# Normalization on GpSimd in a loop of 30 steps: one two-input subtraction for two groups, one multiply for a group, and the bias matmul in one piece

## The chip, the cores and the metric

The kernel runs on one core of a Trainium2 chip. The metric is the device time of one execution in microseconds. Single runs are told by their median; the profile comes from one execution of its own.

## The reference, cut to what matters

The input x is 16 graphs of 512 nodes with 128 channels, float32. Three layers of graph work (normalization, aggregation, a feed-forward product, convolution, message passing and a gated update) come first. Then the last layer runs 30 steps on all 8,192 rows, and it is this loop that the change touches:

```python
def step(h, _):
    h = h + 0.01 * jnp.tanh(h)
    h = h * jax.nn.sigmoid(h)
    h = _layernorm(h, ln_w, ln_b)      # (h - mean) * rsqrt(var + 1e-5) * w + b, over 128 channels
    h = jnp.einsum('bsc,dc->bsd', h, W) + b
    return (h, None)
x, _ = jax.lax.scan(step, x, None, length=N_ITERS)   # 30
```

The result is added to x.

## The kernel before, in words

**Stages.** The graph layers work through the 16 graphs one after the other, in three interleaved phases (`steps`). The first groups of the loop are begun inside the last graph's steps. Then comes the loop itself (`slots`): the 8,192 rows are cut into 64 tiles of 128 rows by 128 channels; eight tiles are a group (`GT`, 1,024 columns on 128 partitions), and eight groups are all the data. One slot is one group of one iteration, 240 slots in all.

**A group's way round.** TensorE multiplies the eight tiles by the weight (`product_group`, L890) into two banks of PSUM. ScalarE takes the tanh (L1010), VectorE forms h + 0.01 tanh(h) (L1326), ScalarE applies the silu and writes the group into its own buffer of `g_ring` (L1000), VectorE gathers sums and squares of each row (`statistics_of`, L1309) and, for two groups at a time, a reciprocal root by a chain of small instructions (`root_link`, L1363 to L1397), whose last one writes `f_rs`. GpSimd normalizes the group from `g_ring` into `h_ring` (`scale`). TensorE transposes the eight tiles (L942), and ScalarE copies them back to SBUF for the next product (L1014).

**Order.** Every engine has its own written order of work per slot. The engines trail one another by fixed lags in groups: the silu by one (`LAG_S`), the negated means by four (`LAG_M`), the scaling by five (`LAG_P`), the transposes by six (`LAG_T`). `h_ring` has four buffers and `f_rs` two. Semaphores (`f_bn`, `f_root`, `f_mean`, `f_norm`, `f_turn`, ...) carry the hand-overs.

**What GpSimd does for a group.** `PLAIN` = 2 of the four tiles in each half of a group are only multiplied by the reciprocal root, in one two-input instruction of 256 columns whose second operand is a column of `f_rs` repeated over 128 channels (L525). The other two tiles of the half take one instruction each (L528): add the negated mean, multiply by the root, both being values per partition. The negated means of two groups come from `less_mean` (L512) once in two slots, ahead of the scaling. After each half the semaphore `f_norm` is raised, so a group raises it twice.

**How the mean of the plain tiles is taken off.** The tiles that were not centred go through the plain weight `w1_t`, whose row for the last channel is used for the bias, and the others through a weight `w1c_t`. The bias of the plain tiles comes in by a matmul in bf16 ahead of the product (`bias`, L906): the bias is split in three bf16 parts in the rows of `bias1`, 256 columns for each half. The centred tiles are transposed with 127 rows, and a row of ones, written once by `ones_row` at the beginning, carries their bias.

**TensorE's slot.** Product of group k; wait for the first half of the group six behind (`f_norm`); two transposes, bias of the first half, two transposes; wait for the second half; two transposes, bias of the second half, two transposes.

Of the kernel before, what the change touches and what calls it, by code (L numbers as in the profile page):

```python
# [27 lines left out]
P = 128  # L28
# [27 lines left out]
EARLY = 7  # L56
PLAIN = 2

# [34 lines left out]
def build(nc, x, adj, w0, b0, wf, bf, w_se, b_se, conv1_w, bn1, conv2_w, bn2, w_msg, b_msg,  # L93
          w_ih, b_ih, w_hh, b_hh, ln_w, ln_b, w1, b1, out):
    with ExitStack() as ctx:
# [17 lines left out]
        f_rs = sb("f_rs", [P, 2, PAIR])  # L113
        f_less = sb("f_less", [P, GROUPS, GT])
        f_share = sb("f_share", [P, PAIR])
# [81 lines left out]
        u_ring = [sb(f"u_ring{r}", [P, GN])[:] for r in range(2)]  # L197
        g_ring = [sb(f"g_ring{r}", [P, GN])[:] for r in range(4)]
        h_ring = [sb(f"h_ring{r}", [P, GN])[:] for r in range(4)]
        g_ring += [sb(f"g_ring{r}", [P, GN])[:] for r in range(4, GROUPS)]  # L200

# [199 lines left out]
        def both(j):  # L401

            return j // 2 % 2

        def pairs(i, j):

            return i * (GROUPS // 2) + j // 2 - BY_POWER // 2
# [54 lines left out]
        def _(pool):  # L462
# [44 lines left out]

            def less_mean(j, s):

                pool.wait_ge(f_bn, s + 2)  # L510
                settle(pool, s_passed_pool)
                pool.tensor_scalar(f_less[:, j:j + 2, :], f_stat[:, j:j + 2, 0, :, 1], -1.0, 1.0,  # L512
                                   ALU.mult, ALU.mult).then_inc(f_mean, 1)

            def scale(i, j, s):
                if isinstance(i, int) and i == 0 and j < BY_POWER:
                    pool.wait_ge(f_pow, j + 1)
                else:
# [12 lines left out]

            def slot(it, k):
                older = earlier(it, k, LAG_M)
                if older is not None and k % 2 == 0:
                    less_mean(*older[1:])
                before = earlier(it, k, LAG_P)
                if before is not None:
                    scale(*before)

            def step(b, p, c, d):  # L540
# [39 lines left out]
                if ends(b, B):  # L580
                    power(2)
                    power(3)
                    less_mean(2, 2)
                if l1:
# [8 lines left out]
                if ends(b, B - 1):  # L593
                    rstd(3, b - 1)
                    power(0)
                    less_mean(0, 0)
                    scale(0, 0, 0)
                    power(1)
                    scale(0, 1, 1)
# [15 lines left out]
        def _(pe):  # L615
# [288 lines left out]

            def bias(k, h):
                pe.matmul(y_ps[(k + 1) % 2][:, h, 0:PLAIN * C], ones_bf[:],  # L906
                          bias1[:, 0:PLAIN, :].rearrange("p t c -> p (t c)"),
                          start=True, stop=False, skip_group_check=True)

            def ones_row(b):  # L910

                for t in range(0, NT, NT - PLAIN):
                    pe.matmul(bank[b][:, C * t:C * t + C * (NT - PLAIN)], ones_bf[:],
                              bias1[:, PLAIN:NT, :].rearrange("p t c -> p (t c)"), start=(t == 0), stop=True,
                              skip_group_check=True)

            def slot(it, k):
# [4 lines left out]
                if before is not None:  # L922
                    i, j, s = before
                    if ends(i, 0) and j == 0:
                        pe.wait_ge(s_conv_pre, B)
                        ones_row(CONV)
                        pe.wait_ge(s_x_nmp_lo, B)
                        ones_row(CHAN)
                    elif ends(i, 0) and j == 1:
                        pe.wait_ge(s_r, B)  # L930
                        ones_row(DIST_A)
                    else:
                        pe.wait_ge(f_state, s - 1)
                    pe.wait_ge(f_norm, 2 * s + 1)
                for n in range(GT):
                    if before is not None:
                        if n == NT:
                            pe.wait_ge(f_norm, 2 * s + 2)
                            wait(pe, f_state, s)
                        t = (n + NT * (j % 2)) % GT  # L940
                        rows = P if t % NT < PLAIN else P - 1
# [204 lines left out]
        def _(dve):  # L1146
# [15 lines left out]
            link(dve.memset(bias1[:], 0.0))  # L1162
            dve.memset(bias1[0:1, PLAIN:NT, :], 1.0)
            dve.memset(b1_cols, 0.0)
# [77 lines left out]
            def split_bias():  # L1242
# [5 lines left out]
                link(dve.tensor_copy(part_bf[:, 2, :], part_f[:, 2, :]))  # L1248
                for t in range(PLAIN):
                    for r in range(3):  # L1250
# [120 lines left out]
            def root_link(n, i, j, s):  # L1371
# [22 lines left out]
                else:  # L1394
                    dve.wait_ge(f_link, done)
                    dve.wait_ge(f_norm, 2 * s - 4)
                    dve.scalar_tensor_tensor(out=f_rs[:, both(j), :], in0=f_share[:], scalar=LESS[2],  # L1397
# [219 lines left out]
```

## Time and profile before

| | us |
|---|---|
| Median of three runs | 1288.19 (1287.89 to 1288.37) |
| The profiled execution's own time | 1290.16 |
| Its span, first to last instruction | 1288.3 |

The profile counts for each engine the time it is busy (PE is TensorE's matmuls, PEld its weight loads, DVE VectorE, ACT ScalarE, POOL GpSimd). Times of single instructions are in nanoseconds where they stand as a mean, otherwise in microseconds. The span leaves out what lies around the instructions. In the loop the granted clock of TensorE is 1.00, its upper level.

### The profile page before, as it was taken

How to read it: one execution, taken by the hardware profiler on the slowest of the kernel's cores; microseconds unless marked ns; L12 is line 12 of the kernel's file. 1: busy time of each engine (PE TensorE's matmuls, PEld its weight loads, DVE VectorE, ACT ScalarE, POOL GpSimd, SP SyncE). 2: the span in 40 equal slices, each digit the busy share in tenths (PEclk: the TensorE clock that was granted, in tenths of full speed). 3: DMA queues.
4: the chain of work that ended last, by engine and by line, in shares of the span. 5: the costliest groups of instructions: out<-in, count | busy, mean ns of one | idle time of the engine just before them, and what ended most of it. 6: DMA issues, size and time to landing. Idle time of an engine off the chain costs nothing.

```text
span 1288.3 us, 30559 instructions
## 1 busy us (share of the span) xinstructions
PE 1250.8 (97%) x9315; PEld 1111.1 (86%) x9315; DVE 1156.3 (90%) x3029; ACT 960.1 (75%) x1170; POOL 991.9 (77%) x1867
## 2 busy tenths in 40 slices
PE   8899999999999999789999999999999999999998
PEld 7677777777777777589999999999999999999998
DVE  7888888888888877889999999999999999999996
ACT  2455555555555555789999999999999999999994
POOL 3455555554555554699999999999999999999997
PEclk9999999999999999889999999999999999999999
DMA  6111111111111000000000000000000000000004
GB/s 192 42 42 44 52 52 53 45 41 41 41 41 41 0 1 1 1 2 1 0 0 0 0 0 0 0 0 0 0 0 0 0 0 0 0 0 0 0 0 131
DMA packets 29811, 27.75 MB, mean 22 GB/s; under 512 B 3285, under 2 KB 21464, under 8 KB 29656
## 3 DMA queue, kind: packets, MB, share of 16 engines
q1 hardware_dynamic: 29784, 27.41, 6.6%
q8 instruction: 15, 0.25, 0.1%
q14 instruction: 12, 0.10, 0.0%
HBM read 23.21 MB, written 4.19 MB: 21 GB/s over the span
## 4 chain that ended last, share of the span: by engine, by line
PE 39%; DVE 5%; issue 5%; POOL 4%; ACT 2%; DVEq 0%; POOLq 0%; ACTq 0%
PE psum L890 24%; PE psum L942 13%; POOL h_ring L528 3%; PE psum L906 3%; ACT t_ring L1010 2%; DVE f_stat L1309 2%; POOL h_ring L525 1%; DVE u_ring L1326 1%; DVE f_share L1363 1%; DVE psum L1368 1%; DVE psum L1379 0%; DVE psum L1382 0%; DVE f_rs L1397 0%; DVEq L1307 0%; DVEq L1320 0%
## 5 line engine op out<-in xcount | busy, mean ns | idle before, releaser
L528 POOL TENSOR_SCALAR h_ring<-g_ring,f_less,f_rs 128x128 f32<-128x128 f32 x960 | 428.1, 457 | 0.0
L1309 DVE BATCH_NORM_STATS2 f_stat<-g_ring 128x6 f32<-128x256 f32 x960 | 393.6, 424 | 2.4 <-ACT g_ring L1000 2.4
L942 PE MATMUL psum<-ident,h_ring 128*128 128x128 f32 (+1 forms) x1920 | 339.6, 279 | 9.6 <-POOL h_ring L528 9.4
L525 POOL TENSOR_TENSOR h_ring<-g_ring,f_rs 128x256 f32<-128x256 f32 x480 | 296.1, 617 | 17.5 <-DVE f_rs L1397 15.4
L1326 DVE SCALAR_TENSOR_TENSOR u_ring<-t_ring,psum 128x1024 f32<-128x1024 f32 x232 | 282.9, 1219 | 28.2 <-ACT t_ring L1010 27.0
L890 PE MATMUL psum<-w_t,y_all 128*128 128x128 f32 x1920 | 293.7, 276 | 0.0
L890 PE MATMUL psum<-w1c_t,y_all 128*128 128x128 f32 x1920 | 293.7, 276 | 0.0
L942 PEld LDWEIGHTS psum<-ident,h_ring 128*128 128x128 f32 (+1 forms) x1920 | 254.2, 167 | 43.4 <-POOL h_ring L528 17.0
L1010 ACT ACTIVATE t_ring<-psum 128x1024 f32<-128x1024 f32 x232 | 237.7, 1025 | 43.1 <-PE psum L890 42.8
L1014 ACT ACTIVATE y_all<-psum 128x1024 f32<-128x1024 f32 x240 | 244.0, 1017 | 15.9 <-PE psum L942 15.9
L890 PEld LDWEIGHTS psum<-w1c_t,y_all 128*128 128x128 f32 x1920 | 253.9, 193 | 0.0
L890 PEld LDWEIGHTS psum<-w_t,y_all 128*128 128x128 f32 x1920 | 253.3, 192 | 0.0
L1000 ACT ACTIVATE g_ring<-u_ring 128x1024 f32<-128x1024 f32 x240 | 251.7, 1049 | 0.6 <-DVE u_ring L1326 0.5
L906 PE MATMUL psum<-bias,ones_bf 65*128 65x256 bf16 x480 | 131.8, 275 | 0.0
L495 POOL TENSOR_SCALAR ln_ve<-ln_stat 128x4 f32<-128x4 f32 x64 | 19.4, 303 | 132.1 <-DVE ln_stat L1261 132.1
L996 ACT ACTIVATE work<-psum 128x512 f32<-128x512 f32 x64 | 34.7, 595 | 96.2 <-PE psum L757 96.1
L675 PE MATMUL psum<-diff_s_h,wt_h 128*128 128x256 f32 x272 | 81.2, 299 | 0.0
L676 PE MATMUL psum<-diff_s_l,wt_h 128*128 128x256 f32 x272 | 76.4, 281 | 0.0
L677 PE MATMUL psum<-diff_s_h,wt_l 128*128 128x256 f32 x272 | 76.3, 280 | 0.0
L497 POOL TENSOR_TENSOR ln_rs<-ln_ve,half_neg 128x4 f32<-128x4 f32 x64 | 71.7, 1120 | 5.3
L501 POOL TENSOR_TENSOR work<-work 128x512 f32<-128x512 f32 x32 | 46.5, 1455 | 32.7 <-DVE xh_mem L1292 25.5
L1363 DVE TENSOR_REDUCE f_share<-psum 128x16 f32<-128x48 f32 x354 | 67.5, 191 | 0.1
(201 smaller groups left out, 2189.8 us busy)
## 6 DMA issues: line engine op xcount, KB each, us to landing
work<-in_adj_dram SPq DMA_DIRECT2D x16, 1024.0 KB, 5.5
x_tok<-in_x_dram SPq DMA_DIRECT2D x16, 256.0 KB, 5.6
out_dram<-y_all SPq DMA_DIRECT2D x7, 512.0 KB, 3.2
work<-in_L_gnn_conv_w_dram SPq DMA_DIRECT2D x1, 1088.0 KB
out_dram<-y_all SPq DMA_DIRECT2D x2, 256.0 KB, 3.6
work<-in_L_gnn_w_ih_dram SPq DMA_DIRECT2D x1, 384.0 KB
work<-in_L_gnn_w_hh_dram SPq DMA_DIRECT2D x1, 192.0 KB
work<-in_L_gnn_W_dram SPq DMA_DIRECT2D x1, 64.0 KB, 5.1
```

The source lines that it names most:

```text
L525: pool.tensor_tensor(tiles(h_ring[j % 4])[:, first:first + PLAIN, :], tiles(g_ring[j])[:, first:first + PLAIN, :], spread(f_rs[:, both(j), ...
L528: ins = pool.tensor_scalar(tiles(h_ring[j % 4])[:, t, :], tiles(g_ring[j])[:, t, :], f_less[:, j, t:t + 1], f_rs[:, both(j), at + t:at + t ...
L675: pe.matmul(dst, lhs[0], rhs[0], start=start, stop=False)
L890: m = pe.matmul(y_ps[k % 2][:, h, C * t:C * t + C], y_all[:, GT * k + NT * h + t, :], w1_t[:] if t < PLAIN else w1c_t[:], start=False, sto ...
L906: pe.matmul(y_ps[(k + 1) % 2][:, h, 0:PLAIN * C], ones_bf[:], bias1[:, 0:PLAIN, :].rearrange("p t c -> p (t c)"), start=True, stop=False, ...
L942: m = pe.transpose(g_ps[j % 2][0:rows, t // NT, P * (t % NT):P * (t % NT) + P], tiles(h_ring[j % 4])[:, t, 0:rows], ident[:])
L1000: act.activation(g_ring[j], u_ring[j % 2], ACT.Silu).then_inc(f_silu, 1)
L1010: act.activation(t_ring[k % 2], src, ACT.Tanh).then_inc(f_tanh, 1)
L1014: act.activation(y_all[:, GT * j:GT * j + GT, :].rearrange("p t c -> p (t c)"), g_ps[j % 2].rearrange("p h n -> p (h n)"), ACT.Copy).then_ ...
L1309: ins = dve.bn_stats(f_stat[:, j, 0, 2 * q:2 * q + 2, :].rearrange("p t w -> p (t w)"), two)
L1326: dve.scalar_tensor_tensor(out=u_ring[k % 2], in0=t_ring[k % 2], scalar=STEP, in1=src, op0=ALU.mult, op1=ALU.add).then_inc(f_u, 1)
L1363: dve.tensor_reduce(f_share[:], rows, AX_X, ALU.mult).then_inc(f_link, 1)
```

## The change

Two things are changed, and the buffers and weights with them.

- GpSimd now centres one half (four tiles, 512 columns) of each group by a subtraction of the mean in place in `g_ring`, for two groups in one instruction (`centre`): the first half of the even group and the second half of the odd one. The mean comes straight from the statistics, repeated over the channels; the buffer and the instruction of the negated means go. Then one multiply covers a whole group of 1,024 columns (`scale`), and `f_norm` is raised once per group. In its slot the scaling comes first, the centring second. The buffers of two groups now lie side by side (`g_pair`), so that one access reaches both halves.
- In TensorE's slot the half that was not centred gets its bias in one matmul of 512 columns (the two rows of tiles of `bias1` read twice), between the fourth and the fifth transpose. The centred half is transposed first, with 127 rows. The wait for GpSimd is one per group, ahead of the first transpose.

```diff
-        g_ring = [sb(f"g_ring{r}", [P, GN])[:] for r in range(4)]
+        g_pair = [sb(f"g_pair{r}", [P, 2, GN]) for r in range(2)]
...
+        g_ring = [g_pair[j // 2][:, j % 2, :] for j in range(GROUPS)]
...
-            def less_mean(j, s):
+            def centre(j, s):
                 pool.wait_ge(f_bn, s + 2)
-                settle(pool, s_passed_pool)
-                pool.tensor_scalar(f_less[:, j:j + 2, :], f_stat[:, j:j + 2, 0, :, 1], -1.0, 1.0,
-                                   ALU.mult, ALU.mult).then_inc(f_mean, 1)
+                two = g_pair[j // 2][:].rearrange("p g n -> p (g n)").rearrange("p (q n) -> p q n", n=N)[:, 0:4:3, :] \
+                    .rearrange("p g (t c) -> p g t c", c=C)
+                means = f_stat[:].rearrange("p g o t w -> p (g o t) w")[:, :, 1].rearrange("p (q t) -> p q t", t=NT)[:, 4 * j:4 * j + 6:5, :] \
+                    .rearrange("p g (t o) -> p g t o", o=1).broadcast_to([P, 2, NT, C])
+                pool.tensor_tensor(two, two, means, ALU.subtract).then_inc(f_mean, 1)
...
-                for h in (j % 2, 1 - j % 2):
-                    first = NT * h
-                    at = GT * (j % 2)
-                    pool.tensor_tensor(tiles(h_ring[j % 4])[:, first:first + PLAIN, :], tiles(g_ring[j])[:, first:first + PLAIN, :],
-                                       spread(f_rs[:, both(j), at + first:at + first + PLAIN], PLAIN, C), ALU.mult)
-                    for t in range(first + PLAIN, first + NT):
-                        ins = pool.tensor_scalar(tiles(h_ring[j % 4])[:, t, :], tiles(g_ring[j])[:, t, :],
-                                                 f_less[:, j, t:t + 1], f_rs[:, both(j), at + t:at + t + 1], ALU.add, ALU.mult)
-                    ins.then_inc(f_norm, 1)
+                at = GT * (j % 2)
+                pool.tensor_tensor(tiles(h_ring[j % 4]), tiles(g_ring[j]),
+                                   spread(f_rs[:, both(j), at:at + GT], GT, C), ALU.mult).then_inc(f_norm, 1)
...
-                older = earlier(it, k, LAG_M)
-                if older is not None and k % 2 == 0:
-                    less_mean(*older[1:])
                 before = earlier(it, k, LAG_P)
                 if before is not None:
                     scale(*before)
+                newer = earlier(it, k, LAG_M)
+                if newer is not None and k % 2 == 0:
+                    centre(*newer[1:])
...
-                                      w1_t[:] if t < PLAIN else w1c_t[:], start=False, stop=True, skip_group_check=True)
+                                      w1c_t[:] if h == centred(k) else w1_t[:], start=(h == centred(k) and t == 0), stop=True, skip_group_check=True)
...
-            def bias(k, h):
-                pe.matmul(y_ps[(k + 1) % 2][:, h, 0:PLAIN * C], ones_bf[:],
-                          bias1[:, 0:PLAIN, :].rearrange("p t c -> p (t c)"),
+            def bias(k):
+                four = bias1[:, 0:2, :].rearrange("p (o t) c -> p o (t c)", o=1).broadcast_to([KB, 2, 2 * C])
+                pe.matmul(y_ps[k % 2][:, 1 - centred(k), :].rearrange("p (o n) -> p o n", o=2), ones_bf[:], four,
                           start=True, stop=False, skip_group_check=True)
...
-                    pe.wait_ge(f_norm, 2 * s + 1)
+                    pe.wait_ge(f_norm, s + 1)
...
-                    if ahead and n % NT == 1:
-                        if n == 1:
-                            bias_free(it, k)
-                        bias(k, n // NT)
+                    if ahead and n == NT - 1:
+                        bias_free(it, k)
+                        bias((k + 1) % GROUPS)
```

`centred(j)` is `j % 2`. The remaining lines fit the counts of `f_norm` to one per group (VectorE's last link of the root waits for `s - 2` instead of `2 * s - 4`) and the rows of ones to the new layout.

## Rows read from the trace of the kernel before

**Rows 1.** The page's first part: busy time, share of the span and instructions of each engine.
```profile
PE 1250.8 (97%) x9315; PEld 1111.1 (86%) x9315; DVE 1156.3 (90%) x3029; ACT 960.1 (75%) x1170; POOL 991.9 (77%) x1867
```

**Rows 2.** Busy time per engine in three stretches, PEclk the granted TensorE clock.
```profile
core 0: us, PE busy (x) PEld busy (x) DVE busy (x) ACT busy (x) POOL busy (x), PEclk, DMA share, GB/s
500.00:540.00 40.00, 31.50 (x167) 24.22 (x165) 30.32 (x53) 31.23 (x43) 22.76 (x26) 0.98 0.00 1
880.00:904.44 24.44, 24.25 (x211) 23.11 (x210) 23.57 (x74) 23.01 (x25) 23.89 (x53) 1.00 0.00 0
904.44:928.88 24.44, 24.25 (x211) 23.12 (x210) 23.54 (x74) 22.99 (x25) 23.90 (x53) 1.00 0.00 0
```

**Rows 3.** Who waited for whom, 700 to 1100 us: total us, times, longest.
```profile
POOL h_ring L525 <- DVE f_rs L1397: 8.0, 27, 0.4
PEld psum L942 <- POOL h_ring L528: 9.9, 37, 0.4
```

**Rows 4.** Timeline of GpSimd, 916 to 926 us: start us, us, engine line op, tiles.
```profile
916.05 0.21 POOL L512 TENSOR_SCALAR f_less<-f_stat 128x16 f32<-128x16 f32 x1
916.22 0.62 POOL L525 TENSOR_TENSOR h_ring<-g_ring,f_rs 128x256 f32<-128x256 f32 x1
916.82 0.89 POOL L528 TENSOR_SCALAR h_ring<-g_ring,f_less,f_rs 128x128 f32<-128x128 f32 x2
...
922.01 0.21 POOL L512 TENSOR_SCALAR f_less<-f_stat 128x16 f32<-128x16 f32 x1
...
925.49 0.61 POOL L525 TENSOR_TENSOR h_ring<-g_ring,f_rs 128x256 f32<-128x256 f32 x1 [0.38 <-DVE f_rs L1397]
```

**Rows 5.** The chain that ended last, one group on TensorE: start us, us, what.
```profile
907.86 1.79 PE psum L890 x16
909.64 0.22 PE psum L942 x2
909.86 0.11 PE psum L906
909.97 0.44 PE psum L942 x4
910.42 0.11 PE psum L906
910.53 0.22 PE psum L942 x2
```

**Rows 6.** Groups of instructions by shape on GpSimd, whole span: xcount, busy us, mean ns.
```profile
L528 POOL TENSOR_SCALAR h_ring<-g_ring,f_less,f_rs 128x128 f32<-128x128 f32 x960 | 428.1, 457 | 0.0
L525 POOL TENSOR_TENSOR h_ring<-g_ring,f_rs 128x256 f32<-128x256 f32 x480 | 296.1, 617 | 17.5 <-DVE f_rs L1397 15.4 <-issue 1.7 <-POOL f_less L512 0.3
L512 POOL TENSOR_SCALAR f_less<-f_stat 128x16 f32<-128x16 f32 x120 | 25.5, 213 | 0.2
L592 POOL TENSOR_TENSOR x_conv_l<-conv_pre,x_conv_h 128x512 fp32r<-128x512 f32 x16 | 20.9, 1306 | 20.2 <-ACT conv_pre L1103 20.2
L551 POOL TENSOR_TENSOR xh_mem<-h_full 128x257 f32<-128x257 f32 x32 | 19.4, 627 | 49.8 <-ACT h_full L1040 43.8 <-DVE xs L1432 6.0
```

**Rows 7.** Timeline of GpSimd in the graph layers: pairs of 257 and of 512 columns.
```profile
197.65 1.19 POOL L551 TENSOR_TENSOR xh_mem<-h_full 128x257 f32<-128x257 f32 x2 [2.63 <-ACT h_full L1040]
201.62 2.63 POOL L558 TENSOR_TENSOR emb_f<-emb_f 105x512 f32<-105x512 f32 x2 [0.75 <-ACT emb_f L1051]
```

**Rows 8.** Groups of matmuls by shape on TensorE: 256 and 512 columns.
```profile
L676 PE MATMUL psum<-diff_s_l,wt_h 128*128 128x256 f32 x272 | 76.4, 281 | 0.0
L676 PE MATMUL psum<-xc_s_l,wt_h 128*128 128x512 f32 x64 | 25.2, 393 | 0.0
```

**Rows 9.** Timeline of GpSimd where the loop begins and where it ends.
```profile
547.26 1.64 POOL L506 TENSOR_TENSOR f_rs<-f_var,half_neg 128x8 f32<-128x8 f32 x1 [0.84 <-DVE f_var L1350]
548.99 0.72 POOL L512 TENSOR_SCALAR f_less<-f_stat 128x16 f32<-128x16 f32 x1
...
1278.08 0.90 POOL L528 TENSOR_SCALAR h_ring<-g_ring,f_less,f_rs 128x128 f32<-128x128 f32 x2
```

More of the change, by code:

```diff
@@ L56 @@
 EARLY = 7
-PLAIN = 2
 SEED_SLOPE = -0.5
@@ L113, in build @@
         f_rs = sb("f_rs", [P, 2, PAIR])
-        f_less = sb("f_less", [P, GROUPS, GT])
         f_share = sb("f_share", [P, PAIR])
@@ L197, in build @@
         u_ring = [sb(f"u_ring{r}", [P, GN])[:] for r in range(2)]
-        g_ring = [sb(f"g_ring{r}", [P, GN])[:] for r in range(4)]
+        g_pair = [sb(f"g_pair{r}", [P, 2, GN]) for r in range(2)]
         h_ring = [sb(f"h_ring{r}", [P, GN])[:] for r in range(4)]
-        g_ring += [sb(f"g_ring{r}", [P, GN])[:] for r in range(4, GROUPS)]
+        g_pair += [sb(f"g_pair{r}", [P, 2, GN]) for r in range(2, GROUPS // 2)]
+        g_ring = [g_pair[j // 2][:, j % 2, :] for j in range(GROUPS)]
         psum = ctx.enter_context(nc.psum_tensor("psum", [P, 8, N], F32))
@@ L403, in both, with centred @@
             return j // 2 % 2
+        def centred(j):
+            return j % 2
         def pairs(i, j):
@@ L582, in step @@
                     power(3)
-                    less_mean(2, 2)
+                    centre(2, 2)
                 if l1:
@@ L595, in step @@
                     power(0)
-                    less_mean(0, 0)
+                    centre(0, 0)
                     scale(0, 0, 0)
@@ L903, in bias_free @@
                     pe.wait_ge(f_u, it * GROUPS + k)
-            def bias(k, h):
-                pe.matmul(y_ps[(k + 1) % 2][:, h, 0:PLAIN * C], ones_bf[:],
-                          bias1[:, 0:PLAIN, :].rearrange("p t c -> p (t c)"),
+            def bias(k):
+                four = bias1[:, 0:2, :].rearrange("p (o t) c -> p o (t c)", o=1).broadcast_to([KB, 2, 2 * C])
+                pe.matmul(y_ps[k % 2][:, 1 - centred(k), :].rearrange("p (o n) -> p o n", o=2), ones_bf[:], four,
                           start=True, stop=False, skip_group_check=True)
             def ones_row(b):
-                for t in range(0, NT, NT - PLAIN):
-                    pe.matmul(bank[b][:, C * t:C * t + C * (NT - PLAIN)], ones_bf[:],
-                              bias1[:, PLAIN:NT, :].rearrange("p t c -> p (t c)"), start=(t == 0), stop=True,
+                for t in range(0, NT, 2):
+                    pe.matmul(bank[b][:, C * t:C * t + 2 * C], ones_bf[:],
+                              bias1[:, 2:4, :].rearrange("p t c -> p (t c)"), start=(t == 0), stop=True,
                               skip_group_check=True)
@@ L926, in slot @@
                         ones_row(CONV)
-                        pe.wait_ge(s_x_nmp_lo, B)
-                        ones_row(CHAN)
                     elif ends(i, 0) and j == 1:
@@ L937, in slot @@
                         if n == NT:
[L938 to L941, printed above, removed]
+                            if ends(i, 0) and j == 0:
+                                pe.wait_ge(s_x_nmp_lo, B)
+                            else:
+                                pe.wait_ge(f_state, s)
+                        t = (n + NT * centred(j)) % GT
+                        rows = P - 1 if n < NT else P
                         m = pe.transpose(g_ps[j % 2][0:rows, t // NT, P * (t % NT):P * (t % NT) + P],
                                          tiles(h_ring[j % 4])[:, t, 0:rows], ident[:])
-                    if ahead and n % NT == 1:
-                        if n == 1:
-                            bias_free(it, k)
-                        bias(k, n // NT)
+                    if ahead and n == NT - 1:
+                        bias_free(it, k)
+                        bias((k + 1) % GROUPS)
                 if before is not None:
@@ L1162, in _ @@
             link(dve.memset(bias1[:], 0.0))
-            dve.memset(bias1[0:1, PLAIN:NT, :], 1.0)
+            dve.memset(bias1[0:1, 2:4, :], 1.0)
             dve.memset(b1_cols, 0.0)
@@ L1248, in split_bias @@
                 link(dve.tensor_copy(part_bf[:, 2, :], part_f[:, 2, :]))
-                for t in range(PLAIN):
+                for t in range(2):
                     for r in range(3):
@@ L1395, in root_link @@
                     dve.wait_ge(f_link, done)
-                    dve.wait_ge(f_norm, 2 * s - 4)
+                    dve.wait_ge(f_norm, s - 2)
                     dve.scalar_tensor_tensor(out=f_rs[:, both(j), :], in0=f_share[:], scalar=LESS[2],
```

## The prediction

> **What bounds the kernel now.** I began with the busy shares [rows 1]. TensorE leads with 97%, but that is a mean over two stages, so I went on to the stretches of the second stage, the loop of 30 iterations [rows 2]. One iteration of eight groups lasts 24.44 us, the same in both stretches shown. In it TensorE is busy 24.25 us, GpSimd 23.90, VectorE 23.54 and ScalarE 22.99. Four engines stand within 6% of one another, so the loop is bound by whichever is slowed first, and no single one can be made faster for much gain.
>
> GpSimd's own timeline shows how little it has to spare. From one L512 at 916.05 to the next at 922.01, with no wait between them, are 5.96 us: that is all GpSimd does for two groups [rows 4]. Four times 5.96 are 23.84 us of the 24.44. The remaining 0.6 us is idle time, mostly before L525, where it waits for VectorE's f_rs: 8.0 us in 400, up to 0.38 us at once [rows 3, 4]. Two groups may take 24.44 / 4 = 6.11 us, so GpSimd's slack is 0.15 us per pair of groups, 2.5%.
>
> TensorE's part is read from the chain: 1.79 us of products, 0.88 us of transposes (0.22 + 0.44 + 0.22), and twice 0.11 us of bias make 2.89 us per group, 23.1 per iteration [rows 5]. The rest of its 24.44 us is waiting that the profile partly shows, for L528 of GpSimd among others [rows 3]. The question is therefore what GpSimd's work for two groups becomes.
>
> **What goes and what comes on GpSimd.** For two groups the change takes away the 5.96 us just read: one f_less (L512), four two-input multiplies of 256 columns (L525, a mean of 617 ns) and eight one-input instructions of 128 columns (L528, a mean of 457 ns) [rows 4, 6]. From start to start an L525 costs 0.60 us (916.22 to 916.82) [rows 4]. It puts in two multiplies of 1,024 columns and one subtraction of 2 x 512 columns, all two-input. Columns are not saved: 2,048 of multiplication and adding stay as they were, and of them the half that was centred and scaled in one instruction is now passed over twice. Three instructions instead of thirteen save starts; 1,024 columns more are paid for.
>
> No row shows a two-input instruction of 1,024 columns on GpSimd. Call its time T, and bound it:
>
> - From below: the step from 16 columns (L512, 213 ns) to 256 (L525, 617 ns) is 404 ns for 240 columns, 1.68 ns each [rows 6]. Carried on, T = 617 + 768 x 1.68 = 1.91 us. This supposes a start of some 0.19 us that long instructions pay once.
> - From above: two instructions of 257 columns take 1.19 us together and two of 512 take 2.63 [rows 7], 0.595 and 1.315 us each. That is 0.72 us for 255 columns more, 2.82 ns each, and T = 1.315 + 512 x 2.82 = 2.76 us. A single 512 with another output (L592) has 1,306 ns [rows 6], so the 512 is no oddity of one line.
> - Between them: four times the 0.60 us of the existing multiply [rows 4], T = 2.40 us. Twice the 512 gives 2.63.
>
> I take 2.40. It is the same multiplication of the same tiles by the same repeated column of f_rs, only in one piece; and the 512-column rows say that a longer instruction saves nothing per column here (2.57 ns against 2.32 at 257), so I expect no gain from length. The subtraction reads a repeated column as the multiply does; I give it the same T.
>
> The Trainium skill, page "GPSIMD Engine Reference", section "Elementwise — side-by-side cycle accounting", gives 4,497 ns for a two-input add of 2,048 columns, and about 2.6 cycles an element. Half of that would be an estimate of T = 2.25 us, and the time by it 1,362 us; the trace's 512 columns at 1.3 us lie above its pace, so the rows keep the say.
>
> **The sum.** Two groups cost GpSimd 3 x 2.40 = 7.20 us against a period of 6.11. No other engine is slowed, so GpSimd becomes the bound alone and its wait for f_rs disappears. In the loop it then runs without a break from 549.0 us, where the last power has ended and the centring of groups 2 and 3 begins (now L512) [rows 9]. From there it has 119 pairs: 238 multiplies and 119 subtractions, 119 x 7.20 = 857 us. Its last instruction ended at 1278.98 us [rows 9], 9.3 us ahead of the end of the span of 1288.3; to that I add 0.45 us, since the transposes of the last group now wait for the whole of it: four of them and a bias, read from the chain, no longer run beside GpSimd's second half [rows 5]. Span: 549.0 + 856.8 + 9.8 = 1415.6 us. The profiled execution took 1290.16 us, 1.86 more than its span; the median of the runs shown is 1288.19, almost exactly the span, so the forecast for the median is 1415.5, rounded **1416 us**, 10% slower.
>
> **Edits at no cost.** The bias in one piece: 256 columns are 0.11 us on the chain [rows 5], and in the first stage 512-column matmuls have a mean of 393 ns against 281 for 256 [rows 8], so 0.11 us more for 256 more. Twice 0.11 stays 0.22. One weight load goes, which runs beside the matmuls. All this lies beside GpSimd's 7.20 us; without that cover the two rows leave 0.22 us against 0.22, within 0.01 us a group either way, some 2 us over 240 groups. The single hand-over per group: TensorE now starts a group's transposes after the whole multiply, with the products, the bias and the other transposes queued behind its wait. While GpSimd is the bound this adds nothing to the period; if T were small, it would cost up to the half of a group that used to be ahead, 1.2 us, but once, as TensorE runs a group behind GpSimd by plan. Centring is queued behind the multiply of the group before, ahead of its pair's own; it waits for the same statistics as L512 did, and VectorE computes f_rs meanwhile. At the start the subtraction for groups 0 and 1 delays the first group by T - 0.21 = 2.2 us, which the idle time before the loop (0.84 us before L506 and more ahead of it) covers in part [rows 9]; 2 us is the risk. The TensorE clock: TensorE would be busy 23.1 of 28.8 us, 80%; a stretch with 79% was granted 0.98 [rows 2], so I add nothing.
>
> **Rivals.**
>
> - **GpSimd is cheap in long pieces (faster).** If T follows the lower line, 1.91 us, two groups cost 5.73 us, under the 5.96 of now. It decides below T = 2.04, a third of 6.11. VectorE's 23.54 us per iteration is then the next bound, 5.89 us a pair [rows 2]: 119 x 0.22 = 26 us less, 3 us back for the start and the last group, so 1265 us. For it speaks that short instructions of 4 to 16 columns already take some 0.2 us, so a start is in every row; against it that the 512-column rows stand 0.25 us above that line. 15%.
> - **The pace of the 512-column rows.** T = 2.63: 3 x 2.63 = 7.89, 119 x 7.89 + 558.8 = 1498 us; at the upper bound 2.76, 1544. For it: they are the longest rows on this engine. Against it: both their operands are full streams; here one is a repeated column. 22% for T above 2.5.
> - **A little slower.** T from 2.06 to 2.2 gives 1294 to 1344 us. It takes a start worth about half of what the lower line supposes. 10%.
> - **No difference.** T around 2.0, where GpSimd takes as long as now, or the hand-over eats a small gain. 3%.
>
> **How the numbers follow.** My forecast, T between 2.2 and 2.5 (1344 to 1451 us), has 50%. Faster by over 0.2%, about what a measurement of this kernel can tell from no change, is the first rival alone: 0.15. Within it 0.03. Slower is all the rest, 0.82. The range leaves out the first rival, the 3%, and the far end of the pace of 512 columns: from 1308 (T = 2.10) to 1498 (T = 2.63), which holds nearly 8 in 10. If slower, the likeliest case by itself is 1344 to 1451.
>
> **What would show it.** In the new profile the multiply of 1,024 columns should have a mean near 2.40 us and the subtraction the same; an iteration should last about 28.8 us, with GpSimd busy over 98% of it and no wait before its multiply. TensorE should wait for GpSimd in every group, some 0.7 us, and VectorE and ScalarE fall to about 82 and 80% busy. A multiply under 2.04 us would make the forecast wrong in its sign; TensorE at a lower granted clock, or GpSimd waiting for f_rs or for the transposes again, would make it wrong in its mechanism.

## The result and the profile after

The changed kernel took a median of 1266.47 us (1266.19 to 1266.96, four runs), the kernel before, on the same chip, 1288.04 (1287.67 to 1288.37): a ratio of 0.9833, interval 0.9816 to 0.985. It is 21.6 us faster, where 128 us slower was forecast; the time lies under my range and within 2 us of the first rival's 1265.

The page's first part and the groups on GpSimd and of the bias after (busy us, mean ns, idle before), against [rows 1, 6]:

```profile
PE 1228.6 (97%) x9073; PEld 1094.2 (86%) x9073; DVE 1151.8 (91%) x3029; ACT 959.6 (76%) x1170; POOL 947.0 (75%) x667
L528 POOL TENSOR_TENSOR h_ring<-g_pair,f_rs 128x1024 f32<-128x1024 f32 x240 | 451.6, 1903 | 34.0 <-DVE f_rs L1395 18.3
L518 POOL TENSOR_TENSOR g_pair<-g_pair,f_stat 128x1024 f32<-128x1024 f32 x120 | 229.6, 1913 | 0.0
L906 PE MATMUL psum<-bias,ones_bf 65*128 65x512 bf16 x240 | 92.0, 384 | 0.0
```

A multiply of 1,024 columns has a mean of 1,903 ns, the subtraction 1,913. My T was 2.40 us. GpSimd's share did not rise, it fell, from 77% to 75% of a shorter span. The bias in one piece costs 92.0 us of TensorE's busy time against 131.8 in two, but these spans overlap with neighbours; what it is worth is measured below.

GpSimd's timeline after, against [rows 4]:

```profile
891.71 3.75 POOL L528 TENSOR_TENSOR h_ring<-g_pair,f_rs 128x1024 f32<-128x1024 f32 x2 [0.54 <-DVE f_rs L1395]
895.42 1.91 POOL L518 TENSOR_TENSOR g_pair<-g_pair,f_stat 128x1024 f32<-128x1024 f32 x1
897.48 3.75 POOL L528 TENSOR_TENSOR h_ring<-g_pair,f_rs 128x1024 f32<-128x1024 f32 x2 [0.16 <-POOL g_pair L518]
901.19 1.91 POOL L518 TENSOR_TENSOR g_pair<-g_pair,f_stat 128x1024 f32<-128x1024 f32 x1
...
915.26 3.75 POOL L528 TENSOR_TENSOR h_ring<-g_pair,f_rs 128x1024 f32<-128x1024 f32 x2 [0.54 <-DVE f_rs L1395]
```

From one subtraction to the next (895.42 to 901.19) are 5.77 us for two groups, where 5.96 stood. From start to start a multiply costs 1.855 us (891.71 to 895.42 for two). Two multiplies and a subtraction are 5.6 us; the rest is 0.16 to 0.22 us in which the multiply waits for GpSimd's own subtraction, or 0.54 us, once in an iteration, for f_rs. An iteration, 891.71 to 915.26, lasts 23.55 us; it was 24.44. Thirty times 0.89 are 27 us. The two profiled spans differ by 23.2 us (1288.3 and 1265.1): about 3 us are given back where the loop begins, its first tanh that waits for TensorE standing at 561.47 us instead of 558.71. (The profiled execution of the kernel before was itself 2 us above its median.)

One iteration after, by engine, against [rows 2]:

```profile
core 0: us, PE busy (x) PEld busy (x) DVE busy (x) ACT busy (x) POOL busy (x), PEclk, DMA share, GB/s
891.71:915.26 23.55, 23.48 (x202) 22.53 (x202) 23.34 (x73) 22.98 (x26) 22.47 (x13) 1.00 0.00 0
```

TensorE is busy 23.48 of 23.55, VectorE 23.34, GpSimd 22.47. Nothing of the forecast is there: GpSimd was to be busy over 98%, and TensorE to wait some 0.7 us in each group.

### The profile page after: what moved, and what is told of

Same layout as the page of the kernel before. It is cut to its first block, busy times and chain, and to the rows that moved or that the text cites. A ratio compares the mean times of both kernels' runs of the same rounds, so it can differ in the third digit from the quotient of the medians.

```text
span 1265.1 us, 28292 instructions
## 1 busy us (share of the span) xinstructions
PE 1228.6 (97%) x9073; PEld 1094.2 (86%) x9073; DVE 1151.8 (91%) x3029; ACT 959.6 (76%) x1170; POOL 947.0 (75%) x667
## 4 chain that ended last, share of the span: by engine, by line
PE 62%; DVE 18%; issue 8%; POOL 5%; ACT 5%; DVEq 1%; DMA 0%; SPq 0%; POOLq 0%; ACTq 0%
PE psum L889 21%; PE psum L941 11%; POOL h_ring L528 4%; PE psum L674 4%; PE psum L676 4%; PE psum L675 4%; PE psum L845 4%; PE psum L696 3%; DVE u_ring L1324 3%; PE psum L691 3%; PE psum L906 3%; ACT t_ring L1008 2%; DVE emb_n L1502 2%; DVE f_stat L1307 2%; DVE xh_mem L1290 1%
## 5 line engine op out<-in xcount | busy, mean ns | idle before, releaser
L528 POOL TENSOR_TENSOR h_ring<-g_pair,f_rs 128x1024 f32<-128x1024 f32 x240 | 451.6, 1903 | 34.0 <-DVE f_rs L1395 18.3
L1307 DVE BATCH_NORM_STATS2 f_stat<-g_pair 128x6 f32<-128x256 f32 x960 | 394.6, 425 | 2.4 <-ACT g_pair L998 2.4
L941 PE MATMUL psum<-ident,h_ring 128*128 128x128 f32 (+1 forms) x1920 | 297.1, 277 | 8.3 <-POOL h_ring L528 6.4
L889 PE MATMUL psum<-w_t,y_all 128*128 128x128 f32 x1920 | 254.4, 276 | 0.0
L889 PE MATMUL psum<-w1c_t,y_all 128*128 128x128 f32 x1920 | 254.2, 275 | 0.0
L998 ACT ACTIVATE g_pair<-u_ring 128x1024 f32<-128x1024 f32 x240 | 251.8, 1050 | 0.9 <-DVE u_ring L1324 0.9
L889 PEld LDWEIGHTS psum<-w_t,y_all 128*128 128x128 f32 x1920 | 234.3, 192 | 0.0
L889 PEld LDWEIGHTS psum<-w1c_t,y_all 128*128 128x128 f32 x1920 | 234.1, 192 | 0.0
L518 POOL TENSOR_TENSOR g_pair<-g_pair,f_stat 128x1024 f32<-128x1024 f32 x120 | 229.6, 1913 | 0.0
L906 PE MATMUL psum<-bias,ones_bf 65*128 65x512 bf16 x240 | 92.0, 384 | 0.0
```

The lines of the kernel that those rows point to most:

```text
L518: pool.tensor_tensor(two, two, means, ALU.subtract).then_inc(f_mean, 1)
L528: pool.tensor_tensor(tiles(h_ring[j % 4]), tiles(g_ring[j]), spread(f_rs[:, both(j), at:at + GT], GT, C), ALU.mult).then_inc(f_norm, 1)
L906: pe.matmul(y_ps[k % 2][:, 1 - centred(k), :].rearrange("p (o n) -> p o n", o=2), ones_bf[:], four, start=True, stop=False, skip_group_che ...
L998: act.activation(g_ring[j], u_ring[j % 2], ACT.Silu).then_inc(f_silu, 1)
L1307: ins = dve.bn_stats(f_stat[:, j, 0, 2 * q:2 * q + 2, :].rearrange("p t w -> p (t w)"), two)
```

## Experiments

Two questions: why T was wrong, and why an iteration got 0.89 us shorter. GpSimd's work fell by 0.19 us for two groups (5.96 to 5.77), 0.76 us in an iteration, so the nearest answer to the second question is that GpSimd's work sets the period (theory A below); that is tested with the others. The diffs are against the changed kernel unless said otherwise. The kernels of the measuring row, of the four pieces, of the full buffer, without centring and without bias were run once each.

### What a two-input instruction costs on GpSimd

**A row of measuring instructions** behind GpSimd's last multiply, four of each kind:

```diff
+            pool.wait_ge(f_turn, ITERS * GROUPS)
...
+                bench(4, lambda o: pool.tensor_tensor(tiles(o)[:, 0:n, :], tiles(a_in)[:, 0:n, :], spread(rs[:, 0:n], n, C), ALU.mult))
...
+                bench(4, lambda o: pool.tensor_tensor(tiles(o)[:, 0:n, :], tiles(a_in)[:, 0:n, :], tiles(b_in)[:, 0:n, :], ALU.mult))
...
+            bench(4, lambda o: pool.tensor_tensor(o[:, 0:512], a_in[:, 0:512], a_in[:, 0:512], ALU.mult))
...
+                bench(4, lambda o: pool.tensor_scalar(o[:, 0:n], c_in[:, 0:n], rs[:, 0:1], rs[:, 1:2], ALU.add, ALU.mult))
```

> The changed kernel with a row of measuring instructions on GpSimd behind its last multiply (four of each kind, nothing else changed). Theory S (a start of about 0.2 us for each two-input instruction, then 1.63 ns a column, whatever the operands): repeated operand 256/512/768/1024 columns 0.60/1.02/1.44/1.86 us from start to start, two full streams the same. Theory R (a repeated operand is cheap, a second full stream is dear): repeated as above, two full streams 0.60 at 256, but 1.3 at 512 and 2.6 at 1024. The one-input instruction with two values per partition: 0.44 us at 128 columns under both; if it has a start of 0.2 us too, about 0.7 at 256.

Groups by shape in that stretch (L627 a repeated second operand, L630 two buffers, L644 one buffer as both operands, L646 one input and two values per partition):

```profile
L627 POOL TENSOR_TENSOR h_ring<-g_pair,f_rs 128x256 f32<-128x256 f32 x4 | 2.3, 616 | 2.6 <-PE psum L977 2.6
L627 POOL TENSOR_TENSOR h_ring<-g_pair,f_rs 128x512 f32<-128x512 f32 x4 | 4.0, 1041 | 0.1
L627 POOL TENSOR_TENSOR h_ring<-g_pair,f_rs 128x1024 f32<-128x1024 f32 x4 | 7.5, 1895 | 0.1
L630 POOL TENSOR_TENSOR h_ring<-g_pair 128x256 f32<-128x256 f32 x4 | 2.8, 724 | 0.1
L630 POOL TENSOR_TENSOR h_ring<-g_pair 128x512 f32<-128x512 f32 x4 | 4.9, 1262 | 0.1
L630 POOL TENSOR_TENSOR h_ring<-g_pair 128x1024 f32<-128x1024 f32 x4 | 9.2, 2338 | 0.1
L644 POOL TENSOR_TENSOR h_ring<-g_pair 128x512 f32<-128x512 f32 x4 | 4.0, 1039 | 0.1
L646 POOL TENSOR_SCALAR h_ring<-g_pair,f_rs 128x128 f32<-128x128 f32 x4 | 1.7, 448 | 0.1
L646 POOL TENSOR_SCALAR h_ring<-g_pair,f_rs 128x512 f32<-128x512 f32 x4 | 3.0, 772 | 0.1
```

The kernel took 1341.09 us with this stretch in it. All three kinds are straight lines. A repeated operand: (1,895 - 616) / 768 = 1.67 ns a column and a start of 190 ns. Two buffers: (2,338 - 724) / 768 = 2.10 ns and 186. One input: (772 - 448) / 384 = 0.84 ns and 340 (256 columns, 556 ns, lie on that line). The same columns of one buffer as both operands cost what a repeated column costs (1,039 ns against 1,041). What makes these two kinds cheaper than two buffers is not shown. Theory R holds, with a smaller difference than I had put on it; theory S falls. It also fits the rows that misled me: the two instructions of 257 columns read both operands from one buffer (the even and the odd columns of h_full, an access that the measuring row does not have) and lie on the first line (190 + 257 x 1.67 = 619 ns, measured 627 [rows 6]); those of 512 read two buffers and lie near the second (186 + 512 x 2.10 = 1,261, measured 1,306).

The Trainium skill, "GPSIMD Engine Reference", section "Elementwise — side-by-side cycle accounting", has 4,497 ns for a two-input add of 2,048 columns. The line for two buffers, carried on beyond its longest row of 1,024 columns, gives 186 + 2,048 x 2.10 = 4,487 ns, so the trace agrees for two buffers, and not for a repeated operand (190 + 2,048 x 1.67 = 3,610 ns).

**The multiply in four pieces of 256:**

```diff
-                pool.tensor_tensor(tiles(h_ring[j % 4]), tiles(g_ring[j]),
-                                   spread(f_rs[:, both(j), at:at + GT], GT, C), ALU.mult).then_inc(f_norm, 1)
+                for t in range(0, GT, 2):
+                    ins = pool.tensor_tensor(tiles(h_ring[j % 4])[:, t:t + 2, :], tiles(g_ring[j])[:, t:t + 2, :],
+                                             spread(f_rs[:, both(j), at + t:at + t + 2], 2, C), ALU.mult)
+                ins.then_inc(f_norm, 1)
```

> The multiply of a group in four pieces of 256 columns in place of one of 1,024; the subtraction stays. Theory S and theory R alike: four starts, 4 x 0.60 = 2.40 us a group, two groups 2 x 2.40 + 1.87 + 0.17 = 6.84 us against 5.89, 119 x 0.95 = 113 us more, about 1379 us. Rival: the 0.60 us of 256 columns came from the one-input instructions that stood between, and the pieces take 1.86 us together: about 1266 us.

1352.59 us beside 1289.6 for the kernel before. The pieces have a mean of 613 ns but follow each other at 0.57; from one subtraction to the next are 6.63 us:

```profile
902.27 1.91 POOL L518 TENSOR_TENSOR g_pair<-g_pair,f_stat 128x1024 f32<-128x1024 f32 x1
904.34 4.61 POOL L529 TENSOR_TENSOR h_ring<-g_pair,f_rs 128x256 f32<-128x256 f32 x8 [0.16 <-PE psum L943]
908.90 1.91 POOL L518 TENSOR_TENSOR g_pair<-g_pair,f_stat 128x1024 f32<-128x1024 f32 x1
```

Put into the sum of my prediction, 119 x 6.63 + 558.8 = 1348 us; the span is 1350.7. The sum was sound while GpSimd alone binds. Starts do count: two groups cost 6.63 us in pieces against 5.77 in one, though 0.21 less than the 6.84 that I expected.

**A full buffer as second operand** (a constant, from the second iteration on, so the rows are not scaled to unit variance):

```diff
+                    pool.tensor_tensor(tiles(h_ring[j % 4]), tiles(g_ring[j]), tiles(flat), ALU.mult).then_inc(f_norm, 1)
```

> From the second iteration on the multiply's second operand is a full buffer of 1,024 columns (a constant) in place of the repeated column, so the rows are not scaled to unit variance. Theory S: 1.86 us as before, about 1266 us. Theory R: 2.6 us a multiply, two groups 2 x 2.6 + 1.87 + 0.17 = 7.24 us, some 115 pairs x 1.35 = 155 us more, about 1421 us.

1363.16 us. The multiply has a mean of 2,370 ns in the loop where the repeated column takes 1,897:

```profile
L534 POOL TENSOR_TENSOR h_ring<-g_pair,flat 128x1024 f32<-128x1024 f32 x120 | 281.9, 2370 | 9.5 <-PE psum L950 7.1 <-POOL g_pair L520 2.4
```

Two groups take 6.73 us (the multiplies of one pair begin at 902.54, of the next at 909.27). So the T = 2.40 of my forecast is nearly the price of this kernel's multiply, and not of the changed one's.

### Why an iteration is shorter

**The old one-input instructions in the new layout** (one multiply of 512 columns, then four of L528's kind; negated means as before, behind the scaling):

```diff
+                pool.tensor_tensor(tiles(h_ring[j % 4])[:, rest:rest + NT, :], tiles(g_ring[j])[:, rest:rest + NT, :],
+                                   spread(f_rs[:, both(j), at + rest:at + rest + NT], NT, C), ALU.mult)
+                for t in range(mine, mine + NT):
+                    ins = pool.tensor_scalar(tiles(h_ring[j % 4])[:, t, :], tiles(g_ring[j])[:, t, :],
+                                             f_less[:, j, t:t + 1], f_rs[:, both(j), at + t:at + t + 1], ALU.add, ALU.mult)
+                ins.then_inc(f_norm, 1)
```

> The changed layout, bias and hand-over, but GpSimd centres and scales the one half by four one-input instructions of 128 columns as before, and multiplies the other half by one two-input instruction of 512 columns. Theory S: 1.02 + 4 x 0.444 = 2.80 us a group, two groups 5.60 + 0.17 = 5.77 us, under the 5.89 of the changed kernel's period, so about 1266 us: what matters is that GpSimd gets under 5.8 us for two groups. Theory R: 1.3 + 1.78 = 3.08, two groups 6.3 us, about 1315 us.

Neither: 1316.68 us, ratio to the kernel before 1.0212 (1.0195 to 1.0229). The multiply of 512 has a mean of 1,044 ns, as the line of a repeated operand gives (the 1.3 us I put down for theory R is the price of two buffers, which this multiply does not have), and GpSimd's work for two groups, wait for f_rs apart, is 5.8 us (893.54 to 899.36), as in the changed kernel. Yet it is 50 us slower:

```profile
900.63 1.04 POOL L528 TENSOR_TENSOR h_ring<-g_pair,f_rs 128x512 f32<-128x512 f32 x1 [1.05 <-DVE f_rs L1399]
901.65 1.74 POOL L531 TENSOR_SCALAR h_ring<-g_pair,f_less,f_rs 128x128 f32<-128x128 f32 x4
903.35 1.05 POOL L528 TENSOR_TENSOR h_ring<-g_pair,f_rs 128x512 f32<-128x512 f32 x1
...
913.44 1.04 POOL L528 TENSOR_TENSOR h_ring<-g_pair,f_rs 128x512 f32<-128x512 f32 x1 [1.32 <-DVE f_rs L1399]
```

GpSimd now stands idle 1.05 us for f_rs. What differs is how long a group takes once f_rs is there: 2.72 us (900.63 to 903.35) against 1.86. That led to theory B: a way leads round all engines, from f_rs through the multiply, the transposes, TensorE's groups, the tanh and VectorE's root back to a later f_rs, and its length sets the period.

In this kernel GpSimd waits for f_rs twice in an iteration of 25.35 us (at 900.63 and 913.44, and so on), and from one such wait to the next the way leads through one group on TensorE. The turn that ends at 900.63 began with the multiply at 888.09; between them stand

```profile
890.90 0.71 PE L945 MATMUL psum<-ident,h_ring 128*127 128x128 f32 x4 [0.94 <-POOL h_ring L531]
894.09 1.03 ACT L1012 ACTIVATE t_ring<-psum 128x1024 f32<-128x1024 f32 x1 [0.76 <-PE psum L893]
```

The 0.86 us by which a group takes longer are thus paid twice, and 1.72 us is nearly all by which the iteration is longer than 23.55.

In the kernel before and in the changed one, the chain that ended last closes once in an iteration, with five groups on TensorE. Before:

```profile
904.02 0.44 PE psum L942 x2
...
906.91 0.61 PE psum L942 x4
...
912.87 0.61 PE psum L942 x4
...
915.93 0.65 PE psum L942 x4
...
916.91 1.80 PE psum L890 x16
...
925.11 0.07 DVE f_rs L1397
...
927.54 0.88 POOL h_ring L528 x2
928.46 0.44 PE psum L942 x2
```

and after, one full turn:

```profile
891.71 1.90 POOL h_ring L528
893.66 0.71 PE psum L941 x4
...
895.02 1.79 PE psum L889 x16
...
905.47 0.56 PE psum L941 x4
...
906.69 1.80 PE psum L889 x16
908.52 1.04 ACT t_ring L1008
...
914.87 0.17 DVE f_rs L1395
915.26 1.90 POOL h_ring L528
```

GpSimd's part of the turn was 925.49 to 928.42, 2.93 us, with the transposes of the first half beside it; it is 1.90 us now. TensorE's part has grown only from 14.69 (904.02 to 918.71) to 14.83 us (893.66 to 908.49). All transposes of that group now stand behind the multiply, 0.6 us more; but before, three times in the five groups four transposes took 0.61 to 0.65 us instead of 0.44, and after only once 0.56. The rest, from TensorE's last product to the next multiply, is 6.78 us before (918.71 to 925.49) and 6.77 after (908.49 to 915.26). Together 0.9 us less. The subtraction is not on this way: it is done while VectorE is still at the root.

**The centring ahead of the multiply in the slot**, the old order:

```diff
+                newer = earlier(it, k, LAG_M)
+                if newer is not None and k % 2 == 0:
+                    centre(*newer[1:])
                 before = earlier(it, k, LAG_P)
                 if before is not None:
                     scale(*before)
-                newer = earlier(it, k, LAG_M)
-                if newer is not None and k % 2 == 0:
-                    centre(*newer[1:])
```

> The changed kernel with the centring put ahead of the multiply in GpSimd's slot, the old order. Theory A (GpSimd's work for two groups binds: 5.57 us of three instructions plus the 0.17 us it waits for its own subtraction): the own wait goes, since another multiply stands between, up to 0.17 x 119 = 20 us faster, about 1250 us. Theory B (the way from f_rs through the multiply to the transposes binds): the multiply of the group before comes 1.86 us later, its transposes wait, about 0.6 us for two groups, 70 us slower at most, about 1290 to 1335 us.

1305.57 us, ratio 1.0132 (1.0115 to 1.0149): the same work, 39 us slower than the changed kernel. The multiply of the group before now waits behind the subtraction (911.73, then 913.59), and GpSimd stands idle later, up to 1.06 us for f_rs:

```profile
909.87 1.90 POOL L528 TENSOR_TENSOR h_ring<-g_pair,f_rs 128x1024 f32<-128x1024 f32 x1 [1.06 <-DVE f_rs L1395]
911.73 1.91 POOL L518 TENSOR_TENSOR g_pair<-g_pair,f_stat 128x1024 f32<-128x1024 f32 x1
913.59 3.92 POOL L528 TENSOR_TENSOR h_ring<-g_pair,f_rs 128x1024 f32<-128x1024 f32 x2
```

So GpSimd's work for two groups does not set the time, and theory A falls. The result lies where theory B has it, and the order of the two lines in the slot is part of the gain.

**The centring left out** (2 of every 128 columns only):

```diff
-                pool.tensor_tensor(two, two, means, ALU.subtract).then_inc(f_mean, 1)
+                pool.tensor_tensor(two[:, :, :, 0:2], two[:, :, :, 0:2], means[:, :, :, 0:2], ALU.subtract).then_inc(f_mean, 1)
```

> The subtraction touches 2 of every 128 columns, so the centring is left out; GpSimd's work for two groups falls from 5.57 to about 3.9 us. Theory A: the next bound is TensorE's dense 2.89 us a group, 23.1 us an iteration against 23.55, about 13 us faster, 1253 us. Theory B: the subtraction lies beside VectorE's work on f_rs and costs nothing, so 1266 us, within 4.

1262.69 us, 3.8 less. In the loop nothing is gained: GpSimd waits 1.8 to 2.2 us for f_rs before each pair, and an iteration (899.16 to 922.71) is 23.55 us as before the edit:

```profile
899.16 3.75 POOL L528 TENSOR_TENSOR h_ring<-g_pair,f_rs 128x1024 f32<-128x1024 f32 x2 [1.92 <-DVE f_rs L1395]
902.87 0.23 POOL L518 TENSOR_TENSOR g_pair<-g_pair,f_stat 128x16 f32<-128x16 f32 x1
...
922.71 3.75 POOL L528 TENSOR_TENSOR h_ring<-g_pair,f_rs 128x1024 f32<-128x1024 f32 x2 [1.91 <-DVE f_rs L1395]
```

The 4 us lie where the loop begins: its first tanh that waits for TensorE stands at 557.34 us, in the changed kernel at 561.47. Two subtractions stand ahead of that point, 1.91 and 2.55 us long. This is theory B, and against theory A: 1.7 us less work of GpSimd for two groups leave the period as it was.

**The kernel before, with one hand-over per group** (diff against before):

```diff
-                    pe.wait_ge(f_norm, 2 * s + 1)
+                    pe.wait_ge(f_norm, 2 * s + 2)
```

> The kernel before, with one edit: TensorE waits for the whole group ahead of the first transpose, as in the changed kernel. My prediction's step (the single hand-over costs 1.2 us at most, and once): about 1290 us. Theory B (one way round the iteration goes through f_rs, the multiply and the transposes): four transposes and a bias, 0.44 + 0.11 + 0.22 = 0.77 us, come behind GpSimd's second half in each iteration instead of beside it, 30 x 0.77 = 23 us slower, about 1311 us.

1320.89 us, ratio 1.0258 (1.0242 to 1.0274), 32.5 us slower; an iteration takes 25.47 us against 24.44. GpSimd waits for f_rs twice in it, as in the kernel with the old instructions; before, the longest such wait was 0.38 us [rows 4]:

```profile
902.50 0.61 POOL L525 TENSOR_TENSOR h_ring<-g_ring,f_rs 128x256 f32<-128x256 f32 x1 [0.74 <-DVE f_rs L1397]
...
915.36 0.61 POOL L525 TENSOR_TENSOR h_ring<-g_ring,f_rs 128x256 f32<-128x256 f32 x1 [0.96 <-DVE f_rs L1397]
```

That is more than theory B's 23 us, which counted the 0.77 us once in an iteration. So the hand-over per half was worth that much in the old arrangement, and giving it up is paid for in the new one by the shorter multiply.

### What holds the period at 23.55 us

| edit of the changed kernel | median us | us an iteration |
|---|---|---|
| none | 1266.47 | 23.55 |
| bias in two matmuls again | 1266.92 | 23.55 |
| bias left out (one run) | 1260.31 | 23.29 |
| multiply of group 4 in two pieces, a hand-over after each | 1267.11 | 23.56 |
| last statistics instruction of a group half as wide | 1264.65 | 23.49 |
| that, and no bias (one run) | 1259.10 | 23.28 |
| the same, with the bias, and group 4 in two pieces | 1267.59 | 23.57 |

(The period is the distance of ScalarE's tanh instructions between 600 and 1200 us, times eight groups; in the last row it is read from GpSimd's timeline, 898.33 to 921.90.) The edits, in the order of the rows (without the bias the products start their bank themselves, and with the pieces the counts of `f_norm` are fitted to them):

```diff
+                for o in range(2):
+                    pe.matmul(y_ps[k % 2][:, 1 - centred(k), 2 * C * o:2 * C * o + 2 * C], ones_bf[:],
+                              bias1[:, 0:2, :].rearrange("p t c -> p (t c)"),
+                              start=(o == 0), stop=False, skip_group_check=True)
...
             def bias(k):
+                return
...
+                if j == 4:
+                    for h in range(2):
+                        pool.tensor_tensor(tiles(h_ring[j % 4])[:, NT * h:NT * h + NT, :], tiles(g_ring[j])[:, NT * h:NT * h + NT, :],
+                                           spread(f_rs[:, both(j), at + NT * h:at + NT * h + NT], NT, C), ALU.mult).then_inc(f_norm, 1)
...
+                if q == 3:
+                    two = two[:, 0:C // 2, :]
```

The bias in two matmuls:

> The changed kernel with the bias again in two matmuls of 256 columns, one after the other at the same place. All theories: 0.22 us on TensorE either way, within 3 us of 1266 us. If a matmul has a start of 0.05 us on the path, 240 x 0.05 = 12 us slower, 1278 us.

It came out as expected, ratio to the kernel before 0.9835 (0.9819 to 0.9852): the one piece of 512 columns is worth nothing by itself in this kernel.

The bias left out (the half that is not centred gets none):

> The bias matmul is left out (the half that is not centred gets no bias), 0.22 us less on TensorE for each group. Theory A: GpSimd's 5.74 us for two groups bind, 22.96 us an iteration against 23.55, about 1249 us at best. Theory B: the way round an iteration holds about five groups of dense TensorE work, 1.1 us less, stopped by GpSimd at 22.96 us, about 1249 us too. If TensorE is off the path: 1266 us.

It gained 6 us of the 17 expected, and an iteration is 0.26 us shorter. GpSimd then runs at 5.78 us for two groups and waits once an iteration for TensorE (up to 0.36 us), TensorE for GpSimd:

```profile
PEld psum L939 <- POOL h_ring L528: 21.4, 52, 0.6
POOL h_ring L528 <- PE psum L939: 11.6, 52, 0.4
```

Group 4 in two pieces:

> The changed kernel with the multiply of group 4 alone, the one whose f_rs comes last in each iteration, in two pieces of 512 columns and a hand-over after each. Theory B: the transposes of that group begin 0.85 us earlier, GpSimd pays 0.13 us more; TensorE's and VectorE's own work (23.1 and 23.3 us an iteration) allows 0.2 us of it, about 1260 us. If VectorE alone sets the period: 1266 us.

No gain (ratio 0.9838, 0.9824 to 0.9852): f_rs comes no earlier. The pieces cost GpSimd 0.14 us (2.04 us for both against 1.90), and the chain of this kernel leads through GpSimd's next multiplies, which are late instead.

Statistics half as wide (of two tiles from 64 of 128 channels):

> The changed kernel with the last of the four statistics instructions of each group reading half its columns (128 in place of 256), 0.13 us less on VectorE for each group, 1.07 us an iteration. The statistics of those two tiles come from 64 of 128 channels. Theory V (VectorE sets the changed kernel's period): down to TensorE's own 23.1 to 23.3 us, 8 to 13 us faster, about 1256 us. Theory T (TensorE's dense work sets it): 1266 us.

1.8 us, not 8 to 13; the period is 0.05 us shorter, 1.6 us in thirty iterations. The wait for f_rs stays:

```profile
889.84 3.75 POOL L528 TENSOR_TENSOR h_ring<-g_pair,f_rs 128x1024 f32<-128x1024 f32 x2 [0.54 <-DVE f_rs L1397]
```

With the bias left out as well:

> The same, and the bias matmul left out too (0.22 us a group off TensorE, 1.76 us an iteration). Theory V and T together: the period falls to GpSimd's 5.74 us for two groups, 22.96 us an iteration, 30 x 0.59 = 18 us faster than the changed kernel, about 1249 us. If GpSimd and its waits already bind: 1260 us, as with the bias left out alone.

1259.10 us, as with the bias left out alone. And without that, but with group 4 in two pieces:

> The split multiply of group 4 and the shorter statistics together, each of which alone left the period at 23.5 us. Two limits at one height (the way round through f_rs and VectorE's own work): each hid the other, together about 23.3 us an iteration, where GpSimd stands, some 7 us faster, 1260 us. TensorE's dense work alone: 23.5 us and 1265 us again.

No gain either. In that kernel the chain leads through GpSimd, from group 4's pieces over the next multiply and subtraction to TensorE. What is shown: no single relief of GpSimd, of VectorE or of the way round moves the period by more than 0.05 us, and less work on TensorE by 0.26. TensorE's dense 2.89 us a group are 23.1 of the 23.55; GpSimd's work with its own waits is 23.1 too (4 x 5.77).

The turn of the changed kernel shown above gives a likely reason, in the last of its five groups:

```profile
902.32 0.52 PEld L941 LDWEIGHTS psum<-ident,h_ring 128*127 128x127 f32 x4
903.31 3.75 POOL L528 TENSOR_TENSOR h_ring<-g_pair,f_rs 128x1024 f32<-128x1024 f32 x2 [0.21 <-POOL g_pair L518]
905.32 0.52 PEld L941 LDWEIGHTS psum<-ident,h_ring 128*127 128x127 f32 x4
```

GpSimd has multiplied that group at 905.21 (903.31 + 1.90), and TensorE, one group of 2.89 us after 902.32, would turn to its transposes at 905.21 as well (it does at 905.32). So a way through GpSimd's own work is as long here as the one through TensorE's groups, and relieving one leaves the other. No run tests this by itself, and which combination would have to go to reach 23.1 stays open. None of the versions that do the whole work beats the changed kernel.

## Why the prediction was wrong

The step that failed is the price of T, and within it this sentence: "the 512-column rows say that a longer instruction saves nothing per column here (2.57 ns against 2.32 at 257), so I expect no gain from length". The two rows are not one kind at two lengths: the 257 columns read one buffer, the 512 two. I saw the difference ("both their operands are full streams; here one is a repeated column") and used it only against the upper rival. The lower bound, 1.91 us from a start of 0.19 us and 1.68 ns a column, was the line of the operation at hand: measured 1.90, start 0.19, 1.67 ns. That it fits so well is partly luck, as its point at 16 columns (L512) is a one-input instruction, another kind. With 1.90 in place of 2.40 GpSimd's work for two groups is 5.6 us and not 7.20, and it does not become the bound alone.

- **GpSimd's old work**, 5.96 us for two groups: right, and so was that the change pays with columns and gains in starts. I did not price the starts of the instructions that go: a one-input instruction has 0.34 us of start in its 0.45, eight of them 2.7 us of the 5.96.
- **The sum**, start and tail and 119 pairs: right where GpSimd binds, within 3 us of the spans of the four-piece kernel (1348 against 1350.7) and of the full-buffer kernel (119 x 6.73 + 558.8 = 1360 against 1361.4).
- **The first rival**, 1265 us at 15%: right in its price of T and in sign. Its time is right by luck: its mechanism, VectorE as the next bound at 23.54 us, is not borne out, as 1.07 us less work on VectorE gave 0.05 us an iteration.
- **The bias at no cost**: right, 1266.92 against 1266.47.
- **The single hand-over**, "1.2 us, but once": wrong. In the kernel before it costs 32.5 us, 1.0 in every iteration, as each iteration takes the way through f_rs again. I also left out what the whole change does to that way: by the two chains the 0.89 us come from the time from f_rs to TensorE, and not from GpSimd's work as a whole.
- **The order in the slot**: I named what is queued behind what, and gave it no price; against the old order it is worth 39 us.
- **The start**, 2 us of risk: 2.8 measured (the tanh at 561.47 against 558.71).
- **The clock** stayed at 1.00 from 605 to 1200 us, but TensorE was not relieved either. In the full-buffer kernel, which comes nearest to the forecast, TensorE was busy 359 us of the 400 from 700 on, and the granted clock was 1.00 too. Where the loop begins (557 to 569 us) it was 0.83, and 0.92 in the kernel before: TensorE had stood idle ahead of it for 6.38 us, and for 4.60 before.

## What to carry to other kernels

Before carrying a price per column from one row to another, see what its operands are: two rows of one operation at two lengths that do not lie on a line with a plausible start may be two kinds (the rows of 257 and 512 columns give 2.82 ns a column and a start below nothing, 0.595 - 257 x 0.00282 = -0.13 us). On an engine that is nearly full, the work for a group and the time from its last input to its output are two different prices; work that can be done before the last input comes (here the centring, ahead of f_rs) can be free, as long as the order of the lines in the slot does not put it ahead of work that others wait for.

## What the hardware showed that I had not expected

All of it is read from 128 or 256 to 1,024 float32 columns on 128 partitions. On GpSimd a two-input instruction whose second operand is a repeated column costs 1.67 ns a column, and 2.10 with two buffers, both with a start of 0.19 us (616 ns at 256 columns and 1,895 at 1,024; 724 and 2,338); the same columns of one buffer as both operands cost as little as the repeated column (1,039 ns at 512). A one-input instruction with two values per partition has a start of 0.34 us and 0.84 ns a column (448 ns at 128 columns, 772 at 512). Instructions of 256 columns back to back follow each other at 0.57 us where each is shown with 0.61.
